# Out-projection of a macaron block in three f16 terms, with contexts split on two engines and routed stores spread over pairs

## The chip, the cores and the metric

The kernel runs on one core of one Trainium2 chip. The time is that of the device, in microseconds (us), median of several runs. The core has a TensorE (PE; its weight loads are listed as PEld), a VectorE (DVE), a ScalarE (ACT), a GpSimd (POOL) and queues for DMA (SP issues most of them). Each engine runs its own instructions in order; semaphores join them.

## The reference, cut to what matters

x has 4 x 512 tokens of 128 numbers. A switch feed-forward layer (8 experts), an attention of 16 heads and the same feed-forward layer again are added to it one after the other:

```
x = x + 0.5 * ffn(layernorm(x))
x = x + attn(layernorm(x))
x = x + 0.5 * ffn(layernorm(x))

# attn, for each of the 4 sequences of 512 tokens
q, k, v = (tanh(x @ W + b) for W, b in ((Wq, bq), (Wk, bk), (Wv, bv)))   # 16 heads of 64
alpha = softmax(where(causal, q @ k.T / 8, -inf))
ctx = alpha @ v                         # all heads side by side: 1024 numbers a token
attn = tanh(ctx @ Wo + bo)              # the out-projection, 1024 -> 128

# ffn
e = argmax(x @ gate_w.T); each expert keeps its first 320 tokens
ans = prob * (relu(x @ w1[e] + b1[e]) @ w2[e] + b2[e])
```

## The kernel before

The span has three stages: the first feed-forward layer (up to about 104 us), the attention (about 110 to 412 us) and the second feed-forward layer. The change is in the attention.

The attention goes over 4 batches b (one sequence of 512 tokens each) and in each over 8 pairs of heads r, so over 32 pairs i = 8b + r. `step(b, r)` exists on each of four engines, written out by hand; a pair is worked on in a pipeline over four steps. In step i:

- PE makes q and k of pair i (`kq`, line 695, three f16 terms: high weights times high x, low times high, high times low), then, where the step has one, the extra work `early`, then the scores of pair i-1 (`scores`, lines 719 and 726), the first half of the contexts of pair i-2 (`context`, lines 758 to 760), v of pair i (lines 705, 706), the transposes of the contexts of pair i-3 (`context_t`, line 554) into the PSUM bank `tT`, and the second half of the contexts of pair i-2.
- ACT does the tanh of q and k, the f16 high half of v (`v_high`), the three exponentials of pair i-1 (`exps`, line 501), the tanh of v, and copies `tT` as f32 into `CT` (`copy_ct`, line 505).
- DVE rounds the exponentials to f16 (`p_high`, line 1085), divides the contexts of pair i-2 by their denominators (`normalise`, lines 1095 and 1099; the denominator is a 65th column of the contexts, made by a column of ones in `Vh`) and makes the low halves of two of the three exponentials (`p_low`, line 1090).
- POOL makes the low half of v (`v_low`) and of the first exponential (`p_low`), both line 360.

There is one bank `tT`, and several things pass through it. Who wants to write into it calls `tt_free(t)`, which waits until `ct_ready` has counted the reading of the transposed contexts of all pairs before t. In step i both `context_t` and, much earlier in the step, `early` wait so, with t = i-3. The `early` work is: in batch 0, steps r = 1, 3, 5, the transposes of the next batch's normalised x (`norm_x`; at r = 1 without the wait); in batches 1 to 3, at r = 3 the out-projection of the batch before (`project_out`, line 775: eight f32 matmuls of 128x128 weights on 512 columns), at r = 4 the transposes of its tanh (`turn_out`, line 783), at r = 6 the transposes of its normalised rows (`turn_batch`, line 554). The last batch has its out-projection behind the last step, in pieces of six, one and one pair.

Beside the pairs, DVE adds the attention's output to x and measures it (r = 4), normalises it (r = 5) and chooses experts (r = 7; ranks and places in r = 0 and r = 1 of the next batch). POOL stores the routed rows of batch b-2 into the dispatch buffer in step r = 3 of batch b = 2 and 3, four indirect DMAs (`dispatch`, line 329) between its `v_low` and its `p_low`; the other two batches are stored behind the steps.

Of the kernel before, what the change touches and what calls it, by code (L numbers as in the profile page):

```python
# [68 lines left out]
B1_COL, BQ_COL, BK_COL, BO_COL, GW_COL, B2_COL, ROWS = 0, 32, 40, 48, 49, 57, 65  # L69
# [18 lines left out]
def macaron(nc, x_d, wq, bq, wk, bk, wv, bv, wo, bo, gate_w, w1, b1, w2, b2, out):  # L88
    ctx = ExitStack()
    with ctx:  # L90
        def sb(name, shape, dt):
            return ctx.enter_context(nc.sbuf_tensor(name, shape, dt))
# [4 lines left out]
        def sem(name):  # L97
# [5 lines left out]
        disp = [nc.dram_tensor(f"disp{k}", [SLOTS + NTOK, ROW], F32, kind="Internal").ap() for k in range(2)]  # L103
# [8 lines left out]
        XN = sb("XN", [P, NT, ROW], F32)  # L112
# [5 lines left out]
        Wf = sb("Wf", [P, 4096], F32)  # L118
# [5 lines left out]
        RT = sb("RT", [P, ROWS], F32)  # L124
# [40 lines left out]
        idx = sb("idx", [P, NT], U32)  # L165
# [11 lines left out]
        am = sb("am", [P, 8], F32)  # L177
        Tq = [sb(f"Tq{u}", [P, GN], F32) for u in range(2)]
        Tk = [sb(f"Tk{u}", [P, GN], F32) for u in range(2)]
        Vh = [sb(f"Vh{u}", [P, GT, 2, HD + 1], F16) for u in range(2)]  # L180
# [7 lines left out]
        bvr, bvt, bvu = Pf0[:, 0, 0:1024], Ph0[:, 0, 0:1024].bitcast(BF16), Ph0[:, 1, 0:1024].bitcast(BF16)  # L188
        rden = [sb(f"rden{h}", [P, GT], F32) for h in range(2)]
        cn = [sb(f"cn{u}", [P, GT, P], F32) for u in range(2)]  # L190
        CT = sb("CT", [P, NPAIR, GN], F32)
        yT = sb("yT", [P, GN], F32)

        SC = ctx.enter_context(nc.psum_tensor("sc", [P, 4, 512], F32))
# [1 line left out]
        pj0, pj1, cx, tT = bank("pj0"), bank("pj1"), bank("cx"), bank("tT")  # L196
# [6 lines left out]
            w1_in0 w1_in1 w2_in0 w2_in1 xe_ps xe_ready h_ps h_ready y_ps yt_ready back_ps y_ready y_sc0 y_sc1  # L203
            combined passed amax amax_all wscale bv_ready w_split w_ready
            q_ps k_ps v_ps tq tk tv v_hi v_lo
            s_ps exp_done p_hi p_lo_v p_lo_p ctx_ps rden_ready ctxn ct_ps ct_ready wo_ps yt yt_ps x_added
            x_hi x_lo""".split()
        S = {n: sem(n) for n in names}
        w1_in, w2_in = [S["w1_in0"], S["w1_in1"]], [S["w2_in0"], S["w2_in1"]]
# [80 lines left out]
        def _(pool):  # L290
# [32 lines left out]
            def dispatch(n, phase, first_tile, tiles):  # L323
                pool.wait_ge(S["idx_ready"], n + 1)
                pool.sem_inc(S["passed"], 1)
                for t in range(tiles):
                    if n == NS - 1 and first_tile + t == NT - 1:
                        pool.sem_inc(S["nearly"], 1)
                    pool.indirect_dma_start(disp[phase], bass.IndirectOffsetOnAxis(ap=idx[:, first_tile + t:first_tile + t + 1], axis=0),  # L329
                                            XN[:, first_tile + t, :], None).then_inc(S["scattered"], 16)  # L330
# [17 lines left out]
            pool.memset(bvf[:], 0.0).then_inc(S["bv_zero"], 1)  # L348
            pool.memset(bvs[:], 0.0).then_inc(S["bvs_zero"], 1)
            for u in range(2):  # L350
                pool.memset(Vh[u][:, :, :, HD:HD + 1], 1.0)
            pool.wait_ge(S["slots_empty"], 16)
            for k, (t0, tiles) in enumerate(FIRST):
                dispatch(k, 0, t0, tiles)
# [11 lines left out]
            def p_low(s, u):  # L366
                pool.wait_ge(S["p_hi"], 3 * s + 1)
                low(Pl[u][:, :, 0:GN], Pf[u][:, :, 0:GN], Ph[u][:, :, 0:GN], S["p_lo_p"])

            def step(b, r, score=True, between=None):  # L370
                i, u = NPAIR * b + r, r % 2
                if score:
                    v_low(i - 1, 1 - u)
                if between:
                    between()
                if score:
                    p_low(i - 1, 1 - u)

            def batch_inv_std(b):
                inv_std(NS + NG + b, 0, GT)  # L380

            def batch_dispatch(b):
                dispatch(NS + b, 1, GT * b, GT)

            inv_std(NS, 0, GT)
            inv_std(NS + 1, 0, GT)
# [5 lines left out]

            for b in range(2, NG):
                for r in range(NPAIR):
                    step(b, r, between={3: lambda: batch_dispatch(b - 2), 4: lambda: batch_inv_std(b - 1)}.get(r))
            step(NG, 0)
            batch_dispatch(NG - 2)
            batch_inv_std(NG - 1)
# [6 lines left out]
        def _(act):  # L405
# [96 lines left out]

            def copy_ct(t, r):
                act.wait_ge(S["ct_ps"], t + 1)
                act.activation(CT[:, r, :], tT[:], ACT.Copy).then_inc(S["ct_ready"], 1)

            def out_tanh(b, ps):
                act.wait_ge(S["wo_ps"], b + 1)
                act.activation(yT[:], ps[:], ACT.Tanh, bias=RT[:, BO_COL:BO_COL + 1]).then_inc(S["yt"], 1)

            def step(b, r, project=True, score=True, turn=True, between=None):
                i, u = NPAIR * b + r, r % 2
# [15 lines left out]
            for b in range(1, NG):  # L528
                between = {3: lambda: out_tanh(b - 1, tT), 6: lambda: copy_xt(NG - 1 + b, 0, tT),
                           7: lambda: exp_logits(NS - 1 + b, 0, GT)}  # L530
# [12 lines left out]
        def _(pe):  # L543
            mm = nc.tensor.matmul
# [136 lines left out]
            TERMS = ((0, 0), (1, 0), (0, 1))  # L681
# [89 lines left out]
            def project_out(b, ps, first=0, end=NPAIR):  # L771

                tt_free(NPAIR * b + end)
                for r in range(first, end):
                    last = mm(ps[:], Wf[:, 3072 + P * r:3072 + P * r + P], CT[:, r, :], start=r == 0, stop=r == NPAIR - 1)  # L775
                if end == NPAIR:
                    last.then_inc(S["wo_ps"], 1)

# [86 lines left out]
        def _(dve):  # L865
# [121 lines left out]
            def scale_weights(s):  # L987
                dve.wait_ge(S["amax_all"], 1)
                s.done(dve.tensor_scalar(am[:, 2:3], am[:, 1:2], 1e-30, None, ALU.max))
                s.done(dve.tensor_scalar(am[:, 3:4].bitcast(U32), am[:, 2:3].bitcast(U32), 0x7F800000, None, ALU.bitwise_and))  # L990
                s.done(dve.reciprocal(am[:, 6:7], am[:, 3:4]))
                s.done(dve.tensor_scalar(am[:, 4:5], am[:, 6:7], 2.0 ** 14, None, ALU.mult))
                s.done(dve.tensor_scalar(am[:, 5:6], am[:, 3:4], 2.0 ** -14, None, ALU.mult))
                s.end()

            dve.memset(carry[:], 0.0).then_inc(S["carry0"], 1)
# [35 lines left out]
            dve.memset(carry[:], 0.0).then_inc(S["carry0"], 1)  # L1032

            dve.wait_ge(S["w_in"], 64)
            s = Steps(dve, S["wscale"], 0, 8)
            s.done(dve.tensor_reduce(am[:, 0:1], Wf[:], X_AXIS, ALU.max))
            s.done(dve.tensor_reduce(am[:, 6:7], Wf[:], X_AXIS, ALU.min))
            s.done(dve.tensor_scalar(am[:, 7:8], am[:, 6:7], -1.0, None, ALU.mult))
# [5 lines left out]
            s = Steps(dve, S["bv_ready"], 0, 8)  # L1044
# [42 lines left out]
            def p_low(s, u, c):  # L1087
                at = scored(s, u, c)[0]
                dve.wait_ge(S["p_hi"], 3 * s + c + 1)
                dve.tensor_tensor(Pl[u][:, :, at], Pf[u][:, :, at], Ph[u][:, :, at], ALU.subtract).then_inc(S["p_lo_v"], 1)  # L1090

            def normalise(c, u, h):
                heads = cx[:, 0:GT * (HD + 1)].rearrange("p (t d) -> p t d", d=HD + 1)
                dve.wait_ge(S["ctx_ps"], 2 * c + h + 1)
                dve.reciprocal(rden[h][:], heads[:, :, HD]).then_inc(S["rden_ready"], 1)
                if h == 0 and not (isinstance(c, int) and c < 2):
                    dve.wait_ge(S["ct_ps"], c - 1)
                dve.wait_ge(S["rden_ready"], 2 * c + h + 1)
                dve.tensor_tensor(cn[u][:, :, HD * h:HD * h + HD], heads[:, :, 0:HD],  # L1099
                                  rden[h][:].unsqueeze(2).broadcast_to([P, GT, HD]), ALU.mult).then_inc(S["ctxn"], 1)  # L1100

            def step(b, r, score=True, mix=True, between=None):
                i, u = NPAIR * b + r, r % 2
                if between:
                    between()
                if score:
                    p_high(i - 1, 1 - u, 0)
                if mix:
                    normalise(i - 2, u, 0)
                if score:  # L1110
                    p_high(i - 1, 1 - u, 1)
                if mix:
                    normalise(i - 2, u, 1)
                if score:
                    p_low(i - 1, 1 - u, 1)
                    p_high(i - 1, 1 - u, 2)
                    p_low(i - 1, 1 - u, 2)

            def add_out(b):

                dve.wait_ge(S["yt_ps"], b + 1)
                xg = X[:, bass.ds(GT * b, GT), :]
                dve.tensor_tensor(xg, xg, tT[:].rearrange("p (t d) -> p t d", d=P), ALU.add).then_inc(S["x_added"], 1)
                dve.wait_ge(S["x_added"], b + 1)
# [5 lines left out]
            for r in range(NPAIR):  # L1130
                def between():
                    if r in X_STATS:
                        x_stats(X_STATS[r])
                    if r in X_TURN:
                        x_low(X_TURN[r])
                    if r in X_APPLY:
                        x_apply(X_APPLY[r])

                step(0, r, score=r > 0, mix=r > 1, between=between)
            dve.wait_ge(S["carry0"], 2)  # L1140

            def batch_stats(b):
# [18 lines left out]
            step(NG, 0, between=lambda: take_ranks(s, NS + NG - 2, GT * (NG - 2), 0, GT, cx))  # L1161
            place(s, GT * (NG - 2), 0, GT)
            normalise(NPAIR * NG - 1, 1, 0)
            normalise(NPAIR * NG - 1, 1, 1)
            add_out(NG - 1)
            batch_stats(NG - 1)
            norm_batch(NG, NG - 1)
# [26 lines left out]
```

## Time and profile before

| | us |
|---|---|
| time before, median of 3 runs | 488.85 (487.86 to 491.42) |
| the profiled execution, its time | 491.53 |
| its span | 489.8 |
| PE busy | 402.5 (82%) |
| DVE busy | 305.4 (62%) |
| ACT busy | 244.9 (50%) |
| POOL busy | 214.6 (44%) |

The span is the time from the first instruction to the last; what lies around it makes up the rest of the execution's time. Shares of busy time are averages over the three stages.

### The profile page before, as it was taken

How to read it: one execution, taken by the hardware profiler on the slowest of the kernel's cores; microseconds unless marked ns; L12 is line 12 of the kernel's file. 1: busy time of each engine (PE TensorE's matmuls, PEld its weight loads, DVE VectorE, ACT ScalarE, POOL GpSimd, SP SyncE). 2: the span in 40 equal slices, each digit the busy share in tenths (PEclk: the TensorE clock that was granted, in tenths of full speed). 3: DMA queues.
4: the chain of work that ended last, by engine and by line, in shares of the span. 5: the costliest groups of instructions: out<-in, count | busy, mean ns of one | idle time of the engine just before them, and what ended most of it. 6: DMA issues, size and time to landing. Idle time of an engine off the chain costs nothing.

```text
span 489.8 us, 11094 instructions
## 1 busy us (share of the span) xinstructions
PE 402.5 (82%) x4555; PEld 299.9 (61%) x4555; DVE 305.4 (62%) x734; ACT 244.9 (50%) x361; POOL 214.6 (44%) x173
## 2 busy tenths in 40 slices
PE   2645999428889999999999978999989988489990
PEld 1432677204667888587878666878577854237760
DVE  5883243655899877479898289798289892301210
ACT  1100454204767788387777456777467731016440
POOL 6463045620544453154434273534174524202787
PEclk9997699855999999999999999999999999779995
DMA  7913343161000000000000010000010001044643
GB/s 219 333 50 90 99 138 107 42 206 81 1 3 2 3 3 2 1 24 2 3 1 3 5 40 3 1 3 3 0 47 1 3 1 44 13 112 120 132 73 28
DMA packets 29194, 24.98 MB, mean 51 GB/s; under 512 B 3082, under 2 KB 25665, under 8 KB 28888
## 3 DMA queue, kind: packets, MB, share of 16 engines
q1 hardware_dynamic: 23008, 17.91, 12.4%
q0 software_dynamic: 4544, 4.22, 4.3%
q10 hardware_dynamic: 1592, 2.14, 1.2%
q8 instruction: 36, 0.59, 0.5%
q14 instruction: 14, 0.11, 0.1%
HBM read 15.29 MB, written 9.51 MB: 51 GB/s over the span
## 4 chain that ended last, share of the span: by engine, by line
PE 52%; DVE 26%; issue 8%; POOL 7%; DMA 4%; ACT 1%; ACTq 1%; SPq 0%; DVEq 0%; POOLq 0%
DVE Pl L1090 7%; PE sc L726 7%; DVE Ph L1085 7%; PE sc L596 7%; PE pj L695 6%; PE tT L775 4%; PE pj L605 4%; PE cx L758 4%; POOL out L342 3%; PE cx L760 3%; PE cx L759 3%; PE pj L705 3%; PE tT L554 3%; POOL disp L329 2%; PE pj L726 2%
## 5 line engine op out<-in xcount | busy, mean ns | idle before, releaser
L726 PE MATMUL sc<-Tq,Tk 64*128 64x128 f32 (+2 forms) x640 | 78.6, 345 | 0.0
L758 PE MATMUL cx<-Vh,Ph 128*128 128x65 f16 x640 | 65.1, 195 | 14.8 <-DVE Pl L1090 7.3
L758 PEld LDWEIGHTS cx<-Vh,Ph 128*128 128x128 f16 x640 | 58.2, 97 | 21.3 <-DVE cn L1099 7.5
L726 PEld LDWEIGHTS sc<-Tq,Tk 64*128 64x128 f32 x640 | 62.3, 187 | 11.6
L1085 DVE CAST Ph<-Pf 128x1024 f16<-128x1024 f32 (+1 forms) x48 | 49.7, 1036 | 31.4 <-ACT Pf L501 31.2
L759 PE MATMUL cx<-Vl,Ph 128*128 128x64 f16 x640 | 64.8, 193 | 0.0
L760 PE MATMUL cx<-Vh,Pl 128*128 128x65 f16 x640 | 64.6, 193 | 0.0
L759 PEld LDWEIGHTS cx<-Vl,Ph 128*128 128x128 f16 x640 | 58.6, 98 | 0.3
L760 PEld LDWEIGHTS cx<-Vh,Pl 128*128 128x128 f16 x640 | 58.7, 97 | 0.0
L428 ACT ACTIVATE hT<-sc,RT 128x320 f32<-128x320 f32 x64 | 33.7, 527 | 44.7 <-PE sc L596 44.0
L360 POOL TENSOR_TENSOR Vl<-Tv,Vh 128x512 f16<-128x512 f32 x16 | 19.4, 1213 | 74.0 <-ACT Vh L493 74.0
L1085 DVE CAST Ph<-Wf 128x1024 f16<-128x1024 f32 (+1 forms) x48 | 45.5, 948 | 5.8 <-ACT Wf L501 5.8
L329 POOL DMA_INDIRECT disp<-XN,idx x32 | 32.7, 1020 | 29.2 <-DVE idx L939 15.9
L596 PE MATMUL sc<-xeT,W 128*128 128x320 f32 x128 | 43.1, 486 | 2.7 <-DVE xeT L951 1.6
L360 POOL TENSOR_TENSOR Pl<-Wf,Ph 128x1024 f16<-128x1024 f32 x16 | 34.7, 2166 | 19.8 <-DVE Ph L1085 19.8
L360 POOL TENSOR_TENSOR Pl<-Pf,Ph 128x1024 f16<-128x1024 f32 x16 | 34.4, 2152 | 17.8 <-DVE Ph L1085 17.6
L479 ACT ACTIVATE Tk<-pj,RT,am 128x512 f32<-128x512 f32 x32 | 24.9, 778 | 33.2 <-PE pj L695 33.2
L501 ACT ACTIVATE Wf<-sc,pshift 128x1024 f32<-128x1024 f32 x32 | 35.6, 1114 | 10.3 <-PE sc L726 7.6
L1090 DVE TENSOR_TENSOR Pl<-Pf,Ph 128x1024 f16<-128x1024 f32 (+1 forms) x32 | 39.0, 1220 | 0.6
L549 PE MATMUL cx<-lower,onesb 128*128 128x512 bf16 x58 | 20.0, 519 | 23.4 <-DVE ve L880 14.0
L726 PE MATMUL pj<-Tq,Tk 64*128 64x128 f32 x256 | 38.8, 272 | 0.0
L963 DVE TENSOR_TENSOR Y<-cx,XE 128x256 f32<-128x256 f32 x16 | 6.8, 424 | 51.0 <-PE cx L616 40.5
(196 smaller groups left out, 1028.9 us busy)
## 6 DMA issues: line engine op xcount, KB each, us to landing
W<-in_L_ffn_w SPq DMA_DIRECT2D x32, 256.0 KB, 2.7
disp<-empty SPq DMA_DIRECT2D x2, 1300.0 KB, 7.6
XE<-disp SPq DMA_DIRECT2D x16, 130.0 KB, 2.3
ytok<-empty SPq DMA_DIRECT2D x1, 1024.0 KB
G<-ytok SPq DMA_DIRECT2D x4, 256.0 KB, 3.4
out<-X SPq DMA_DIRECT2D x4, 256.0 KB
XR<-disp SPq DMA_DIRECT2D x16, 32.5 KB, 2.0
X<-in_L_attn_states SPq DMA_DIRECT2D x2, 256.0 KB, 3.2
```

The lines of the kernel that those rows point to most:

```text
L329: pool.indirect_dma_start(disp[phase], bass.IndirectOffsetOnAxis(ap=idx[:, first_tile + t:first_tile + t + 1], axis=0), XN[:, first_tile + ...
L360: pool.tensor_tensor(dst, src, hi, ALU.subtract).then_inc(done, 1)
L428: act.activation(hT[e % 2][:, ft, :], hbank[ft][:, 0:CAP], ACT.Relu, bias=RT[:, B1_COL + k:B1_COL + k + 1]).then_inc(S["h_ready"], 1)
L501: act.activation(Pf[u][:, :, at], source, ACT.Exp, scale=0.125, bias=pshift[:]).then_inc(S["exp_done"], 1)
L596: mm(hbank[ft][:, 0:CAP], W1[e % 2][:, P * ft:P * ft + P], xeT[e % 2][:], start=True, stop=True).then_inc(S["h_ps"], 1)
L695: last = mm(ps[:], wpart(w, wl, r), (XL if xl else XH)[:, bass.ds(GN * b, GN)], start=t == 0, stop=t == 2)
L726: m = mm(score_bank(h, c)[:, o + x:o + y], Tk[u][half(h), q:q + P], Tq[u][half(h), q + x:q + y], start=False, stop=last and (c, h) != (2, 0))
L758: mm(cx[:, o:o + HD + 1], Ph[u][:, h, a:a + P], Vh[u][:, kt, h, :], start=kt == 0, stop=False)
L759: mm(cx[:, o:o + HD], Ph[u][:, h, a:a + P], Vl[u][:, kt, h, :], start=False, stop=False)
L760: last = mm(cx[:, o:o + HD + 1], Pl[u][:, h, a:a + P], Vh[u][:, kt, h, :], start=False, stop=kt == qt)
L1085: dve.tensor_copy(Ph[u][:, :, at], Pf[u][:, :, at]).then_inc(S["p_hi"], 1)
L1090: dve.tensor_tensor(Pl[u][:, :, at], Pf[u][:, :, at], Ph[u][:, :, at], ALU.subtract).then_inc(S["p_lo_v"], 1)
```

## The change

Four things are changed, all in the attention.

1. The out-projection uses the f16 halves of its weights (`WH`, `WL`, which are scaled by a power of two and are made anyway) in three terms, 24 f16 matmuls of 512 columns in place of 8 f32 ones for each batch.
2. The transposed contexts are split: ACT copies `tT` into an f16 buffer `CTH` and counts `ct_hi`; DVE then subtracts it from `tT` into an f16 buffer `CTL` (`ct_low`) and only that counts `ct_ready`. There is one `ct_low` for each of the 32 pairs, at the end of DVE's step.
3. The column of ones in `Vh` becomes 1/1024, so that contexts are 1024 times larger; the tanh of the out-projection takes a scale that undoes both factors, a column of `am` made by one more small DVE instruction.
4. The four routed stores of a batch are issued one each in steps 2, 3, 4 and 5, behind `p_low`, and no longer together in step 3 ahead of it.

```diff
-        CT = sb("CT", [P, NPAIR, GN], F32)
+        CTH = sb("CTH", [P, NPAIR, GN], F16)
+        CTL = sb("CTL", [P, NPAIR, GN], F16)
...
-                pool.memset(Vh[u][:, :, :, HD:HD + 1], 1.0)
+                pool.memset(Vh[u][:, :, :, HD:HD + 1], 1.0 / CTX_SCALE)
...
                 if score:
                     p_low(i - 1, 1 - u)
+                if behind:
+                    behind()
...
+            def dispatch_tile(b, t):
+                if t == 0:
+                    pool.wait_ge(S["idx_ready"], NS + b + 1)
+                at = GT * b + t
+                pool.indirect_dma_start(disp[1], bass.IndirectOffsetOnAxis(ap=idx[:, at:at + 1], axis=0),
+                                        XN[:, at, :], None).then_inc(S["scattered"], 16)
...
-                    step(b, r, between={3: lambda: batch_dispatch(b - 2), 4: lambda: batch_inv_std(b - 1)}.get(r))
+                    step(b, r, between=(lambda: batch_inv_std(b - 1)) if r == 4 else None,
+                         behind=(lambda: dispatch_tile(b - 2, r - 2)) if 2 <= r < 2 + GT else None)
...
-                act.activation(CT[:, r, :], tT[:], ACT.Copy).then_inc(S["ct_ready"], 1)
+                act.activation(CTH[:, r, :], tT[:], ACT.Copy).then_inc(S["ct_hi"], 1)
...
-                act.activation(yT[:], ps[:], ACT.Tanh, bias=RT[:, BO_COL:BO_COL + 1]).then_inc(S["yt"], 1)
+                act.activation(yT[:], ps[:], ACT.Tanh, bias=RT[:, BO_COL:BO_COL + 1], scale=am[:, 7:8]).then_inc(S["yt"], 1)
...
-                    last = mm(ps[:], Wf[:, 3072 + P * r:3072 + P * r + P], CT[:, r, :], start=r == 0, stop=r == NPAIR - 1)
+                    for k, (wl, cl) in enumerate(TERMS):
+                        last = mm(ps[:], wpart(3, wl, r), (CTL if cl else CTH)[:, r, :],
+                                  start=(r, k) == (0, 0), stop=(r, k) == (NPAIR - 1, 2))
...
+            def ct_low(t):
+                dve.wait_ge(S["ct_hi"], t + 1)
+                dve.tensor_tensor(CTL[:, t % NPAIR, :], tT[:], CTH[:, t % NPAIR, :], ALU.subtract).then_inc(S["ct_ready"], 1)
+
...
                     p_low(i - 1, 1 - u, 2)
+                if turn:
+                    ct_low(i - 3)
...
             normalise(NPAIR * NG - 1, 1, 0)
+            ct_low(NPAIR * NG - 2)
             normalise(NPAIR * NG - 1, 1, 1)
+            ct_low(NPAIR * NG - 1)
             add_out(NG - 1)
```

How the instructions of DVE stand in steps r = 3 and r = 4 of batch 1, from the second `p_high` of step 3 to the addition of the attention's output, before:

```order
L1085 CAST Ph<-Pf 128x2x512 [waits ctx_ps,exp_done]
L1095 RECIPROCAL rden<-cx 128x4 [waits ctx_ps]
L1099 TENSOR_TENSOR cn<-cx,rden 128x4x64 [waits rden_ready]
L1090 TENSOR_TENSOR Pl<-Pf,Ph 128x2x512 [waits p_hi]
L1085 CAST Ph<-Pf 128x2x256 [waits ctx_ps,exp_done]
L1090 TENSOR_TENSOR Pl<-Pf,Ph 128x2x256 [waits p_hi]
L1123 TENSOR_TENSOR X<-X,tT 128x512 [waits yt_ps]
L871 MEMSET spare 128x1 [waits x_added]
```

and with the change:

```order
L1100 CAST Ph<-Pf 128x2x512 [waits ctx_ps,exp_done]
L1110 RECIPROCAL rden<-cx 128x4 [waits ctx_ps]
L1114 TENSOR_TENSOR cn<-cx,rden 128x4x64 [waits rden_ready]
L1105 TENSOR_TENSOR Pl<-Pf,Ph 128x2x512 [waits p_hi]
L1100 CAST Ph<-Pf 128x2x256 [waits ctx_ps,exp_done]
L1105 TENSOR_TENSOR Pl<-Pf,Ph 128x2x256 [waits p_hi]
L1119 TENSOR_TENSOR CTL<-tT,CTH 128x512 [waits ct_hi]
L1144 TENSOR_TENSOR X<-X,tT 128x512 [waits yt_ps]
L885 MEMSET spare 128x1 [waits x_added]
```

The subtraction into `CTL` is the last instruction of the step, behind both low halves. PE waits for `ct_ready` at the out-projection (r = 3 of batch 1), here before:

```order
L695 MATMUL pj<-XH,WL 128x512
L695 MATMUL pj<-XL,WH 128x512
L775 MATMUL tT<-CT,Wf 128x512 [waits ct_ready]
L775 MATMUL tT<-CT,Wf 128x512 x7
L719 MATMUL sc<-maskn,identb 128x128 [waits exp_done]
```

and with the change:

```order
L707 MATMUL pj<-XH,WL 128x512
L707 MATMUL pj<-XL,WH 128x512
L788 MATMUL tT<-CTH,WH 128x512 [waits ct_ready]
L788 MATMUL tT<-CTH,WL 128x512
L788 MATMUL tT<-CTL,WH 128x512
L788 MATMUL tT<-CTH,WH 128x512
```

The wait stands at the same place, behind `kq` and ahead of the scores; what signals it is now the last instruction of DVE's step. POOL in steps r = 2 to 5 of batch 2, before:

```order
L360 TENSOR_TENSOR Pl<-Wf,Ph 128x2x512 [waits p_hi]
L360 TENSOR_TENSOR Vl<-Tv,Vh 128x512 [waits v_hi]
L329 DMA disp<-XN,idx 4608x130 [waits idx_ready]
L329 DMA disp<-XN,idx 4608x130 x3
L360 TENSOR_TENSOR Pl<-Pf,Ph 128x2x512 [waits p_hi]
L360 TENSOR_TENSOR Vl<-Wf,Vh 128x512 [waits v_hi]
L321 TENSOR_TENSOR r<-ve,mhalf 128x4 [waits var_ready]
L360 TENSOR_TENSOR Pl<-Wf,Ph 128x2x512 [waits p_hi]
```

and with the change:

```order
L362 TENSOR_TENSOR Pl<-Wf,Ph 128x2x512 [waits p_hi]
L393 DMA disp<-XN,idx 4608x130 [waits idx_ready]
L362 TENSOR_TENSOR Vl<-Tv,Vh 128x512 [waits v_hi]
L362 TENSOR_TENSOR Pl<-Pf,Ph 128x2x512 [waits p_hi]
L393 DMA disp<-XN,idx 4608x130
L362 TENSOR_TENSOR Vl<-Wf,Vh 128x512 [waits v_hi]
L323 TENSOR_TENSOR r<-ve,mhalf 128x4 [waits var_ready]
L362 TENSOR_TENSOR Pl<-Wf,Ph 128x2x512 [waits p_hi]
L393 DMA disp<-XN,idx 4608x130
```

Nothing stands between `v_low` and `p_low` of step 3 any more.

## Rows read from the trace of the kernel before

**Rows 1.** Busy time by stretch: from:to, length, each engine's busy us, granted clock, DMA.

```profile
153.10:236.30 83.20, 82.68 (x1252) 66.32 (x1249) 62.01 (x111) 61.11 (x83) 36.07 (x22) 1.00 0.02 5
236.30:310.80 74.50, 68.69 (x1019) 54.56 (x1016) 58.87 (x112) 48.75 (x67) 33.52 (x21) 1.00 0.03 9
```

**Rows 2.** Chain of waits: start, us, work; out-projections and the kq three steps later.

```profile
199.57 6.87 PE tT L775 x16
...
228.52 1.29 PE pj L695 x6
...
269.65 6.87 PE tT L775 x16
...
303.01 1.30 PE pj L695 x6
...
344.14 6.87 PE tT L775 x16
...
375.60 1.29 PE pj L695 x6
```

**Rows 3.** Instruction groups by shape: count, busy us, mean ns, idle before.

```profile
L775 PE MATMUL tT<-CT,Wf 128*128 128x512 f32 x48 | 21.1, 592 | 0.0
L695 PE MATMUL pj<-XL,WH 128*128 128x512 f16 x64 | 25.3, 395 | 0.0
L1073 DVE TENSOR_TENSOR XL<-tT,XH 128x512 f16<-128x512 f32 x4 | 2.7, 687 | 4.4 <-ACT XH L456 4.4
L456 ACT ACTIVATE XH<-tT 128x512 f16<-128x512 f32 x4 | 2.4, 595 | 20.0 <-PE tT L554 19.9
```

**Rows 4.** Timeline (start, duration) at the out-projection of batch 1: ACT, PE, DVE.

```profile
197.54 0.59 ACT L505 ACTIVATE CT<-tT 128x512 f32<-128x512 f32 x1
199.41 0.59 PE L775 MATMUL tT<-CT,Wf 128*128 128x512 f32 x1
200.46 0.69 DVE L1090 TENSOR_TENSOR Pl<-Wf,Ph 128x512 f16<-128x512 f32 x1
```

**Rows 5.** Timeline at step r = 6 of batch 1, and its step 5 ahead.

```profile
223.10 1.49 POOL L360 TENSOR_TENSOR Vl<-Tv,Vh 128x512 f16<-128x512 f32 x1 [1.64 <-ACT Vh L493]
223.53 1.08 DVE L888 TENSOR_TENSOR ra<-r 128x4 f32<-128x4 f32 x1
231.57 0.69 DVE L1090 TENSOR_TENSOR Pl<-Pf,Ph 128x512 f16<-128x512 f32 x1
229.65 0.60 PE L554 MATMUL tT<-identf,XN 128*128 128x128 f32 x4
```

**Rows 6.** Timeline at the routed stores of batch 2, r = 3: POOL, DVE, PE.

```profile
279.14 1.20 POOL L329 DMA_INDIRECT disp<-XN,idx  x1 [0.19 <-issue]
...
283.40 1.86 POOL L329 DMA_INDIRECT disp<-XN,idx  x1 [0.30 <-issue]
284.80 4.26 DVE L1090 TENSOR_TENSOR Pl<-Pf,Ph 128x512 f16<-128x512 f32 x1
285.29 2.14 POOL L360 TENSOR_TENSOR Pl<-Pf,Ph 128x1024 f16<-128x1024 f32 x1
289.32 0.19 PE L758 MATMUL cx<-Vh,Ph 128*128 128x65 f16 x1 [2.13 <-DVE Pl L1090]
```

**Rows 7.** Timeline at step r = 5 of batch 0: PE, then DVE.

```profile
154.30 0.38 PE L554 MATMUL tT<-identf,xa 128*128 128x128 f32 x2
...
156.22 0.69 DVE L1090 TENSOR_TENSOR Pl<-Wf,Ph 128x512 f16<-128x512 f32 x1
156.83 0.68 DVE L1073 TENSOR_TENSOR XL<-tT,XH 128x512 f16<-128x512 f32 x1
```

**Rows 8.** The tail: chain piece of the last out-projection, then timeline of DVE and PE.

```profile
399.63 5.23 PE pj L775 x12
...
402.03 0.69 DVE L1090 TENSOR_TENSOR Pl<-Wf,Ph 128x512 f16<-128x512 f32 x1
...
410.18 0.70 PE L775 MATMUL pj<-CT,Wf 128*128 128x512 f32 x1 [0.69 <-ACT CT L505]
```

**Rows 9.** Busy time by stretch, columns as in the first group.

```profile
116.00:122.00 6.00, 5.64 (x35) 3.85 (x35) 3.49 (x19) 2.89 (x5) 0.00 (x0) 0.55 0.00 0
416.00:422.00 6.00, 2.96 (x25) 1.90 (x23) 2.98 (x15) 0.83 (x2) 0.12 (x1) 0.99 0.01 3
422.00:428.00 6.00, 1.79 (x11) 0.66 (x8) 1.75 (x13) 0.00 (x0) 2.56 (x3) 0.50 0.08 24
```

More of the change, by code:

```diff
@@ L59 @@
 ROUTE_STEPS = 12
+CTX_SCALE = 2.0 ** 10
 KOFF = [0, 512, 1024, 896]
@@ L205, in macaron @@
             q_ps k_ps v_ps tq tk tv v_hi v_lo
-            s_ps exp_done p_hi p_lo_v p_lo_p ctx_ps rden_ready ctxn ct_ps ct_ready wo_ps yt yt_ps x_added
+            s_ps exp_done p_hi p_lo_v p_lo_p ctx_ps rden_ready ctxn ct_ps ct_hi ct_ready wo_ps yt yt_ps x_added
             x_hi x_lo""".split()
@@ L368, in p_low, with step @@
                 low(Pl[u][:, :, 0:GN], Pf[u][:, :, 0:GN], Ph[u][:, :, 0:GN], S["p_lo_p"])
-            def step(b, r, score=True, between=None):
+            def step(b, r, score=True, between=None, behind=None):
                 i, u = NPAIR * b + r, r % 2
@@ L993, in scale_weights @@
                 s.done(dve.tensor_scalar(am[:, 5:6], am[:, 3:4], 2.0 ** -14, None, ALU.mult))
+                s.done(dve.tensor_scalar(am[:, 7:8], am[:, 5:6], 1.0 / CTX_SCALE, None, ALU.mult))
                 s.end()
@@ L1034, in _ @@
             dve.wait_ge(S["w_in"], 64)
-            s = Steps(dve, S["wscale"], 0, 8)
+            s = Steps(dve, S["wscale"], 0, 9)
             s.done(dve.tensor_reduce(am[:, 0:1], Wf[:], X_AXIS, ALU.max))
@@ L1100, in normalise, with step @@
                                   rden[h][:].unsqueeze(2).broadcast_to([P, GT, HD]), ALU.mult).then_inc(S["ctxn"], 1)
-            def step(b, r, score=True, mix=True, between=None):
+            def ct_low(t):
+                dve.wait_ge(S["ct_hi"], t + 1)
+                dve.tensor_tensor(CTL[:, t % NPAIR, :], tT[:], CTH[:, t % NPAIR, :], ALU.subtract).then_inc(S["ct_ready"], 1)
+            def step(b, r, score=True, mix=True, turn=True, between=None):
                 i, u = NPAIR * b + r, r % 2
@@ L1137, in between @@
                         x_apply(X_APPLY[r])
-                step(0, r, score=r > 0, mix=r > 1, between=between)
+                step(0, r, score=r > 0, mix=r > 1, turn=r > 2, between=between)
             dve.wait_ge(S["carry0"], 2)
```

## The prediction

> **What bounds the kernel now.** I read the busy time by stretch first. In the stretch that holds most of batches 0 and 1, PE is busy 82.7 of 83.2 us at a granted clock of 1.00, in the next 68.7 of 74.5 [rows 1]. So in batches 0 and 1 every wait that PE gets in the attention is paid in full, and in batches 2 and 3 nearly so. The chain of waits says where the rest went: from the start of the out-projection to `kq` of step 6 it takes 28.95 us in batch 1 (199.57 to 228.52), 33.36 in batch 2 and 31.46 in batch 3 [rows 2]. The work is the same but for the routed stores, so these cost 4.4 and 2.5 us. How they do it stands in the timeline: POOL's `p_low` comes late, behind the four stores, and then runs from 285.29 to 287.43; DVE's last low half, which takes 0.69 us elsewhere, takes 4.26 and ends at 289.06; PE waits 2.13 us for it [rows 6].
>
> Last I looked at who frees `tT`. At the out-projection of batch 1 PE starts at 199.41 straight behind `kq`; ACT's copy of the bank had ended at 198.13, but DVE's step ends only at 201.15 [rows 4]. That is the place the change touches.
>
> **The change, part by part.**
>
> *The matmuls.* Eight f32 matmuls take 6.87 us [rows 2], 0.86 each. An f16 one of the same shape: six of `kq` take 1.29 us [rows 2], 0.215 each, so 24 take 5.2. Gain 1.7 for each of batches 0 to 2, 5.1 in all. In the tail the first six f32 ones take 5.23 [rows 8] and 18 f16 ones 3.9, gain 1.3; the last pair gains 0.2 to 0.3.
>
> *ACT.* The copy into f16 takes 595 ns [rows 3], into f32 0.59 us [rows 4]: nothing. The tanh keeps its form but for a column as scale, the small DVE instruction for that column comes in the first expert stage, once: 0 to 0.2 us, I take nothing. The constant in `Vh` costs nothing.
>
> *`ct_low` as work on DVE.* Its form (one operand in PSUM, one f16 in SBUF, 512 columns, f16 out) is in the trace: 687 ns [rows 3], and the next instruction follows 0.61 us after the start of one that takes 0.69 [rows 7]. 30 of the 32 go on the end of DVE's steps. DVE is busy 62.0 of 83.2 us [rows 1], so most of them lie in idle time. Where DVE is itself late, at r = 7, 0 and 1 (expert choice, ranks, places), I count 0.5 us at each of the two batch boundaries and 0.6 at the tail: the small two-operand instructions there are held by POOL as `ra` is at r = 5, 1.08 us until POOL's subtraction has ended [rows 5], and what is issued 0.6 later is held 0.6 less.
> What would change this is `ct_low` being held by POOL too; the 687 ns are a mean over only four. The Trainium skill (GPSIMD Engine Reference, Specifications) says that the interface to SBUF is shared with VectorE for instructions in a two-port mode or with two SBUF inputs; by that `ct_low`, with one input in PSUM, is free of it, and the trace agrees with 687 ns.
>
> *`ct_low` as what frees `tT`.* PE's early work now waits for the end of DVE's previous step plus one subtraction. Each place, from the end of DVE's last low half (next start 0.08 before that end), plus 0.69, plus 0.04 for the signal:
> - r = 3, batch 1: last low half starts at 200.46, `ct_low` at 201.07, ends 201.76, PE at 201.80 instead of 199.41 [rows 4]: 2.4 us. In batches 2 and 3 DVE comes out of its late stretch, 2.7 each. Sum 7.8.
> - r = 4, three times. After the wait at r = 3 the scores are as late as PE is, so DVE's step starts as late, and nothing of the wait has been used up: again 2.4 each, 7.2.
> - r = 6, three times. DVE's step 5 is longer by the normalising: last low half at 231.57, `ct_low` from 232.18 to 232.87, PE at 232.91 instead of 229.65 [rows 5]: 3.3 each, 9.8.
> - r = 5 of batch 0: DVE runs without a gap there, so the `ct_low` of step 3 comes on top: 156.22 + 0.61, then `ct_low` from 157.44 to 158.13; PE at 158.17 instead of 154.30 [rows 7]: 3.9. At r = 3 of batch 0 nothing has to be freed yet.
> - tail: the first six terms wait for the `ct_low` of the last full step: 402.03 + 0.6 + 0.61, to 403.93; PE at 403.97 instead of 399.47 [rows 8]: 4.5, of which 0.6 is the boundary above.
> - last pair: PE already waits 0.69 for ACT's copy [rows 8]; a `ct_low` of 0.69 and its signal come behind the copy, less 0.3 for the faster matmuls: +0.4.
>
> In each case the queue behind the wait is PE's whole step, scores first; ACT, DVE and POOL live on those scores, so the wait shifts all four engines and nobody catches it up.
>
> *The routed stores.* Moved behind `p_low`, they give back the 4.4 and 2.5 us. POOL is idle 1.64 us ahead of its `v_low` even at r = 5 [rows 5], and a store takes 1.2 to 1.9 us of it [rows 6]; as a store may push `v_low` onto DVE's normalising at r = 5, I take 0.4 off for each batch: gain 4.0 and 2.1. Bounds: nothing, and 6.9.
>
> *Sum.* Waits 7.8 + 7.2 + 9.8 + 3.9 + 4.5 + 0.4 = 33.6; batch boundaries 2 x 0.5 = 1.0; matmuls -5.1 - 1.3 = -6.4; stores -6.1. Total +22. On the profiled execution 491.53 + 22.1 = 513.6; that execution lies 2.7 above the median of its kernel, so the median should come to 488.85 + 22.1 = 511.0.
>
> **The rivals.**
>
> *A. The waits are there, and the clock falls too.* PE gets gaps of 2.4 to 4.5 us, where batch 2's largest so far was 2.13 [rows 6]. The clock is granted at 0.99 from 416 to 422 us, where PE is busy 2.96 of 6 us, and at 0.50 behind [rows 9]; so a few thin microseconds are enough somewhere. Against it: the stretch 236 to 311 holds gaps too and stays at 1.00 [rows 1]. The price: with PE busy 5.64 of 6 us, the clock is still 0.55 from 116 to 122 [rows 9], after a start at 112.8, so that stretch alone loses 0.45 x 6 = 2.7 us, and one fall costs 3 us or more. Three falls give about 520. The Trainium skill (TensorE: Matmul & The Clock Gate, Part 1) has the same rule, that an idle engine goes back to 1.2 GHz and has to be busy for a while to get 2.4 again; by it the longest gaps, at r = 6, at r = 5 of batch 0 and in the tail, are those at risk. Chance 0.18.
>
> *B. The waits are half as long.* If DVE's step were to get shorter once PE is late (its `p_high` is held by POOL's `p_low`, which could drift apart), each wait would shrink, by up to 1 us of ten: about 501. Against it: the collision follows from the first `p_high`, which starts both. Chance 0.1.
>
> *C. The other sign: the bank is not missed.* If DVE's step ended ahead of PE's early work, only the gains would stand: 488.85 - 6.4 - 6.1 + about 1.6 at the boundaries = 478. It turns on one comparison, DVE's step end plus 0.7 against PE's `kq` end; it would need DVE to be 2.4 us earlier at r = 3 and 3.3 at r = 6. The trace has it at 201.15 against 199.41, in PE-bound steps that repeat. Chance 0.04.
>
> **How the numbers follow.** Forecast 0.68, A 0.18, B 0.1, C 0.04. The forecast's own range is 506 to 518: stores between nothing and 6.9 us of gain move it by +6 to -1, the boundaries by 1, and each of the eleven waits may be off by 0.3. The range given goes from 501 (B in) to 521 (three falls of the clock). One per cent of the time is about what a measurement of this kernel tells from no change: slower by over 1% holds the forecast, A and B, 0.95; same 0.02 and faster 0.03 share C.
>
> **What would show it.** In the changed profile: PE's first `project_out` and `turn_out` matmuls and the `turn_batch` transposes idle 2.4, 2.4 and 3.3 us with DVE's `CTL` subtraction as releaser, once per batch; about 4 us ahead of the last out-projection; eleven such gaps and about 33 us in all. Out-projection of a batch 5.2 us. `ct_low` 0.69 us each whatever POOL does. The long 4.26 us low half gone. From `project_out` to `kq` of step 6 batches 2 and 3 as long as batch 1. I am wrong if PE's idle ahead of the early work names something else or is under 1 us; if the clock row has a 0.5 inside the attention, it is A.

## The result, and the profile after

| | before | changed |
|---|---|---|
| time, median of 4 runs | 488.36 (487.31 to 491.42) | 525.12 (522.87 to 529.37) |
| span of the profiled execution | 489.8 | 523.2 |
| attention: first `kq` to the transposes of the last out-projection | 299.8 | 336.4 |
| the same without its start (see below) | 270.2 | 309.0 |

The ratio is 1.075 (95% interval 1.067 to 1.084). By the medians the change makes the kernel 36.8 us slower. The two profiled executions are 33.4 us apart; their attentions differ by 36.6, and the rest of the span is 3.2 shorter in the changed one. The direction was forecast, the size was not: 511 was forecast, with a range that ended at 521.

The attention begins at half clock, and the moment at which the clock rises differs between executions. So its start, from the first `kq` to the first transposes of contexts (`cn`), takes different times with the same 294 matmuls, here in before, in the changed kernel and in the run fill below (length, busy us of PE, PEld, DVE, ACT, POOL, then clock, DMA share, GB/s):

```profile
112.70:142.30 29.60, 25.70 (x294) 18.57 (x294) 23.19 (x67) 19.70 (x26) 10.82 (x8) 0.85 0.01 3
111.00:138.40 27.40, 23.42 (x294) 17.01 (x294) 23.15 (x67) 19.55 (x26) 10.69 (x8) 0.95 0.01 2
110.70:140.70 30.00, 26.07 (x294) 18.93 (x294) 23.24 (x67) 19.70 (x26) 11.21 (x8) 0.84 0.01 2
```

Nothing that any of the kernels changes on this path has begun there, but for POOL's order in three of them. What a kernel costs is therefore read behind the start: 309.0 against 270.2, 38.8 us.

Who waited for whom, PE's waits for DVE's subtraction in the changed kernel (total us, times, longest):

```profile
PE tT L566 <- DVE CTL L1119: 12.4, 4, 3.1
...
PE tT L788 <- DVE CTL L1119: 7.5, 3, 2.6
...
PE tT L797 <- DVE CTL L1119: 6.7, 3, 2.2
PE pj L788 <- DVE CTL L1119: 5.2, 2, 3.8
```

None of these lines exists before. Twelve waits, 31.8 us, at the forecast places. The chain of waits goes through them; here the three steps of batch 1 that have one, r = 3, 4 and 6 (start, us, work):

```profile
202.71 0.69 DVE CTL L1119
203.54 5.34 PE tT L788 x24
...
217.86 0.61 DVE CTL L1119
218.51 0.66 PE tT L797 x4
...
238.34 0.69 DVE CTL L1119
239.07 0.66 PE tT L566 x4
```

The out-projection takes 5.34 us for 24 matmuls, where [rows 2] had 6.87 for the 8 f32 ones (each stands as two records in that row). The subtraction itself is as cheap as [rows 3] said. Its line, over all 32 (min/median/max ns):

```profile
L1119 DVE TENSOR_TENSOR CTL<-tT,CTH x32: 676/683/690, 145.2 to 444.6; 128x512 f16<-128x512 f32 x32
```

What the sum did not have is in the granted clock, the third column from the end:

```profile
158.00:218.40 60.40, 55.95 (x862) 44.25 (x860) 43.41 (x70) 42.39 (x57) 22.42 (x14) 1.00 0.01 2
218.40:224.00 5.60, 5.49 (x55) 4.60 (x56) 2.85 (x14) 1.47 (x2) 1.77 (x3) 0.70 0.16 47
239.00:244.30 5.30, 5.22 (x46) 4.30 (x47) 0.71 (x2) 2.32 (x4) 1.12 (x1) 0.68 0.00 0
284.30:291.40 7.10, 7.06 (x29) 3.01 (x30) 0.00 (x0) 0.04 (x1) 0.00 (x0) 0.76 0.00 0
432.60:439.30 6.70, 6.63 (x20) 2.68 (x21) 1.02 (x8) 0.00 (x0) 3.79 (x4) 0.61 0.09 30
111.00:447.40 336.40, 289.55 (x4088) 223.80 (x4089) 241.93 (x497) 196.99 (x269) 125.46 (x82) 0.94 0.02 7
```

```profile
219.60:223.62 4.02, 4.02 (x31) 3.30 (x31) 2.40 (x13) 1.11 (x1) 1.01 (x1) 0.60 0.22 65
209.26:211.72 2.46, 2.46 (x32) 2.08 (x31) 0.10 (x1) 2.07 (x3) 1.12 (x1) 1.00 0.00 0
```

Ten of the eleven waits over 2 us have such a stretch behind them; only the one at 203.5 has none. Before, the attention had no fall of the clock once the first pairs were under way, not behind its 2.13 us of [rows 6] either; this is all of it behind the start:

```profile
142.30:412.50 270.20, 254.08 (x3762) 200.97 (x3763) 207.56 (x399) 177.06 (x243) 118.38 (x75) 1.00 0.03 8
```

### The profile page after: what moved, and what is told of

Read it like the earlier page. It is cut to its first block, busy times and chain, and to the rows that moved or that the text cites. A ratio compares the mean times of both kernels' runs of the same rounds, so it can differ in the third digit from the quotient of the medians.

```text
span 523.2 us, 11189 instructions
## 1 busy us (share of the span) xinstructions
PE 407.5 (78%) x4587; PEld 302.1 (58%) x4587; DVE 316.8 (61%) x767; ACT 245.1 (47%) x361; POOL 210.8 (40%) x173
## 3 DMA queue, kind: packets, MB, share of 16 engines
q1 hardware_dynamic: 23008, 17.91, 11.8%
## 4 chain that ended last, share of the span: by engine, by line
PE 42%; DVE 34%; issue 10%; POOL 6%; DMA 4%; ACT 2%; ACTq 1%; SPq 0%; DVEq 0%; POOLq 0%
DVE Ph L1100 11%; DVE Pl L1105 10%; PE sc L738 8%; PE sc L608 6%; PE pj L617 4%; PE tT L788 4%; POOL out L344 3%; DVE CTL L1119 3%; PE cx L770 3%; PE tT L566 2%; PE pj L707 2%; PE cx L772 2%; PE cx L771 2%; POOL disp L331 2%; PE pj L738 2%
## 5 line engine op out<-in xcount | busy, mean ns | idle before, releaser
L738 PE MATMUL sc<-Tq,Tk 64*128 64x128 f32 (+2 forms) x640 | 86.3, 372 | 0.0
L738 PEld LDWEIGHTS sc<-Tq,Tk 64*128 64x128 f32 x640 | 67.7, 204 | 14.6 <-issue 5.5
L608 PE MATMUL sc<-xeT,W 128*128 128x320 f32 x128 | 39.6, 454 | 2.7 <-DVE xeT L965 1.6
L738 PE MATMUL pj<-Tq,Tk 64*128 64x128 f32 x256 | 40.2, 278 | 0.0
L513 ACT ACTIVATE Pf<-sc,pshift 128x1024 f32<-128x1024 f32 x32 | 35.2, 1111 | 7.2 <-PE sc L738 5.0
L362 POOL TENSOR_TENSOR Vl<-Wf,Vh 128x512 f16<-128x512 f32 x16 | 18.4, 1150 | 45.9 <-ACT Vh L505 45.9
L617 PE MATMUL pj<-hT,W 128*128 128x320 f32 x128 | 36.8, 433 | 0.0
```

The source lines that it names most:

```text
L362: pool.tensor_tensor(dst, src, hi, ALU.subtract).then_inc(done, 1)
L513: act.activation(Pf[u][:, :, at], source, ACT.Exp, scale=0.125, bias=pshift[:]).then_inc(S["exp_done"], 1)
L608: mm(hbank[ft][:, 0:CAP], W1[e % 2][:, P * ft:P * ft + P], xeT[e % 2][:], start=True, stop=True).then_inc(S["h_ps"], 1)
L617: last = mm((pj0, pj1)[e % 2][:, 0:CAP], W2[e % 2][:, ft, :], hT[e % 2][:, ft, :], start=ft == 0, stop=ft == FT - 1)
L738: m = mm(score_bank(h, c)[:, o + x:o + y], Tk[u][half(h), q:q + P], Tq[u][half(h), q + x:q + y], start=False, stop=last and (c, h) != (2, 0))
```

## The experiments

Fourteen kernels beside the two were tried in five groups; three that bear on one point each are told in a sentence, and the others are in the table. Each group ran on one chip with the kernel before, whose median was between 486.6 and 493.2 there; so times are compared by their ratio, and the attention of the one profiled execution by its length. The table gives both, and in the last column the attention behind its start.

| kernel | median, before beside it | ratio (95%) | attention | behind the start |
|---|---|---|---|---|
| before | 488.4 | 1 | 299.8 | 270.2 |
| changed | 525.1, 488.4 | 1.075 (1.067 to 1.084) | 336.4 | 309.0 |
| fill | 513.3, 487.1 | 1.052 (1.044 to 1.059) | 322.0 | 292.0 |
| low_mid | 497.3, 487.1 | 1.024 (1.016 to 1.031) | 306.8 | 278.1 |
| no_low | 475.7, 487.1 | 0.977 (0.971 to 0.983) | 286.5 | 256.7 |
| stores_only | 480.5, 487.1 | 0.986 (0.980 to 0.992) | 291.6 | 264.1 |
| stores_back | 532.0, 493.2 | 1.077 (1.070 to 1.085) | 343.0 | 313.1 |
| early_late | 502.2, 493.2 | 1.017 (1.009 to 1.024) | 314.2 | 284.5 |
| work_only | 479.6, 486.6 | 0.988 (0.981 to 0.994) | 291.7 | 264.2 |
| wait_only | 510.0, 486.6 | 1.048 (1.041 to 1.056) | 324.5 | 295.8 |
| wait_fill | 505.2, 486.6 | 1.039 (1.034 to 1.045) | 317.4 | 287.5 |
| mid_swap | 481.8, 488.3 | 0.988 (0.981 to 0.996) | 292.4 | 265.5 |
| stores_swap | 481.5, 493.0 | 0.982 (0.973 to 0.991) | 292.2 | 265.3 |

**Theory clock:** the forecast's sum holds, and the time above it is matmuls at half clock behind the waits. **Theory work:** the sum is wrong elsewhere; DVE's 30 more subtractions cost more than the batch boundaries.

### Filler in the waits

```diff
+            def fill(i, count):
+                pe.wait_ge(S["exp_done"], 3 * (i - 1))
+                for k in range(count):
+                    mm(sc[k % 4], onesb[:], lower[:].unsqueeze(1).broadcast_to([P, GT, P]), start=True, stop=True)
...
+                    if turn and i > 3:
+                        fill(i, {3: 10, 4: 9, 5: 13, 6: 13}[r])
                     if turn:
                         tt_free(i - 3)
```

> The changed kernel, with filler: ahead of each wait for the freed bank (r = 3, 4, 6 of batches 1 to 3, r = 5 of batch 0, tail) PE runs 9 to 14 bf16 matmuls of 512 columns into score banks that are free then; they are overwritten. The waits stay, only PE is busy in them. Theory clock: of the time lost, some 17 us are matmuls run at half clock just behind each wait (in the trace of the changed kernel the scores behind a wait take 3.2 to 4.0 us against 2.46 elsewhere, the out-projection 6.7 to 7.0 against 5.3, the tail's 6.6 against 3.9); with filler the granted clock stays 1.00 in the attention and the time falls from 525 to about 508. Theory work: the loss beyond the waits is DVE's added work and collisions; then the time stays at 525 (up to 2 more for the filler).

The attention takes 322.0 us, 14.4 less, and the whole 11.8 less. But here the start took 30.0 us and in the changed kernel 27.4; behind it 292.0 are left of 309.0, 17.0 less. The changed kernel with the waits filled:

```profile
110.70:432.70 322.00, 301.83 (x4211) 228.19 (x4212) 243.16 (x497) 197.18 (x269) 126.25 (x82) 0.99 0.02 7
203.00:224.00 21.00, 20.54 (x240) 13.98 (x239) 10.24 (x27) 9.70 (x13) 6.22 (x5) 1.00 0.05 14
```

The clock stays up (the 0.99 is the start of the attention, before the clock has risen), and nothing else became faster: DVE still frees the bank last, PE only works meanwhile. Theory clock holds for 17.0 us, 1.7 for each of ten falls. What is left is 292.0 - 270.2 = 21.8 us above the kernel before.

### The wait without the work

```diff
                     if turn:
                         tt_free(i - 3)
+                    if turn and i > 3:
+                        pe.wait_ge(S["p_lo_v"], 2 * (i - 2) + 2)
                     early()
```

This is the kernel before with spread stores, f32 out-projection and no subtraction; only the early work (and the last out-projection) waits for DVE's last low half.

> The wait without the work and without any f16 term: the kernel before with spread stores (attention 291.6 us, 480.5 in all), whose early work at r = 3, 4, 6, at r = 5 of batch 0 and in the tail waits in addition for DVE's last low half of the step before. The waits come out of the trace of before: 1.8 us at r = 3 and r = 4 (six), 2.65 at r = 6 and at r = 5 of batch 0 (four), 3.3 in the tail, 24.7 in all. Theory clock: some falls of the clock come on top, 1.5 us each; attention 316 plus up to 12. Without falls, 316.

> As wait_only, with 7 to 13 filler matmuls ahead of each wait, so that PE is not idle in it. Theory clock: granted clock 1.00 throughout the attention, which takes 291.6 + 24.7 = 316, whatever wait_only took beyond that goes away. Were the rest of wait_only's loss something else, both take the same.

wait_only takes 324.5 us in the attention, wait_fill 317.4, against 316 from the rows of the kernel before. Behind the start it is 295.8 and 287.5, against 264.1 in stores_only, the same kernel without the waits. So the waits are 23.4 us, forecast 24.7 (PE's idle times at the eleven places add up to 23.5), and the clock costs another 8.3, again 1.7 for each fall. Here it fell five times, behind the waits of 2.5 us at r = 6 and at r = 5 of batch 0 and of 3.2 in the tail, and never behind the six of 1.7 at r = 3 and 4. The mean clock of the whole attention, and of a stretch in it:

```profile
110.30:434.80 324.50, 288.71 (x4055) 223.88 (x4056) 223.60 (x465) 197.29 (x269) 126.96 (x82) 0.96 0.02 8
158.00:236.00 78.00, 72.87 (x1094) 57.17 (x1090) 53.82 (x99) 52.55 (x71) 29.33 (x18) 1.00 0.02 5
```

The second stretch holds the first waits of 1.7 us, at 202.4 and 218.6, and its clock is 1.00.

### The work without the wait, and the gain alone

no_low leaves the subtraction out, and with it the low halves of the contexts, and lets ACT's copy free the bank:

```diff
-                act.activation(CTH[:, r, :], tT[:], ACT.Copy).then_inc(S["ct_hi"], 1)
+                act.activation(CTH[:, r, :], tT[:], ACT.Copy).then_inc(S["ct_ready"], 1)
...
-                        last = mm(ps[:], wpart(3, wl, r), (CTL if cl else CTH)[:, r, :],
+                        last = mm(ps[:], wpart(3, wl, r), CTH[:, r, :],
```

> The changed kernel without the subtraction into CTL; the high halves stand in for the low ones in the third term, and ACT's copy frees the bank as before. It leaves out the low halves of the contexts. All else (24 f16 matmuls, spread stores, scale) is as changed. Both theories: this is the gain alone, 6.4 us of matmuls and up to 6.9 of stores, time 488.4 - 6.4 - 6.1 = about 476; were it at 485 or more, the gains that the prediction counted would be smaller than said.

Measured 475.7 and an attention of 286.5: behind the start, the gain of the change without its subtraction is 13.5 us (forecast 12.5). work_only adds to no_low, at the place of each subtraction in a step, an instruction that frees nothing:

```diff
+                dve.tensor_reduce(busy[:, t:t + 1], G[:, 0:GT, :].rearrange("p t d -> p (t d)"), X_AXIS, ALU.max)
```

> Takes the two jobs of the subtraction apart: the work without the wait. The changed kernel, but ACT's copy frees the bank as before, and at the place of each subtraction DVE runs a maximum over 512 f32 numbers of SBUF, with one input, about as long. It leaves out the low halves of the contexts, as no_low does (attention there 286.5 us, start of the first kq to the transposes of the last out-projection). Theory wait: the work is hidden but for the batch boundaries, attention 287 to 289. Theory work: 30 x 0.6 = 18 us more, attention above 295.

It takes 677 ns each and 291.7 us in the attention, 5.2 more than no_low; behind the start it is 264.2, 7.5 more. Neither theory had that number: more than half of the work is hidden (7.5 of 30 x 0.61 = 18 us shows), but it costs over four times the 1.6 us counted for the boundaries. The changed kernel has about the same work on DVE and takes 309.0. So about 45 us of its loss come from who frees the bank and not from the work: the waits, and the clock behind them.

### The stores

stores_only is the kernel before with the fourth part of the change alone; stores_back is the changed kernel without it:

```diff
-                    step(b, r, between=(lambda: batch_inv_std(b - 1)) if r == 4 else None,
-                         behind=(lambda: dispatch_tile(b - 2, r - 2)) if 2 <= r < 2 + GT else None)
+                    step(b, r, between={3: lambda: batch_dispatch(b - 2), 4: lambda: batch_inv_std(b - 1)}.get(r))
```

> The kernel before with the routed stores of batches 0 and 1 spread over r = 2 to 5 behind p_low, nothing else. As the prediction counts them: 4.0 + 2.1, time 482.3. Rival: the stores collide with other work and the gain is under 2 us.

> The changed kernel with its routed stores together again in r = 3 of batches 2 and 3, ahead of p_low. By the prediction's terms they cost 6.1 us, 525.1 + 6.1 = 531; alone on the kernel before they cost 6.6. Rival: here PE waits at r = 4 in any case, so the stores hide behind that wait, and the time stays at 525 to 527.

Alone, the spread stores take 8.2 us off the attention, of which 2.1 are the earlier rise of the clock in its start and 6.1 the stores, and 1.4% (0.8 to 2.0) off the whole. Undone in the changed kernel they put 6.6 back in the attention, 336.4 to 343.0, but only 4.1 behind the start, 309.0 to 313.1, and by their ratios, 1.075 and 1.077, the two kernels can't be told apart. The clock fell eight times in stores_back and ten times in the changed kernel, which at 1.7 us each hides some 3 us; what the stores cost in the changed kernel is open between 4 and 8. The rival, that PE's wait at r = 4 hides them, is at least not the whole: the late low half of [rows 6] makes the subtraction late too, and PE waits up to 3.8 us for it there:

```profile
PE tT L796 <- DVE CTL L1118: 8.4, 3, 3.8
```

This line is of stores_back; with spread stores the same three waits are 6.7 us, the longest 2.2.

### Moving the subtraction

low_mid puts it ahead of the two low halves of DVE's step:

```diff
                 if mix:
                     normalise(i - 2, u, 1)
+                if turn:
+                    ct_low(i - 3)
                 if score:
                     p_low(i - 1, 1 - u, 1)
...
                     p_low(i - 1, 1 - u, 2)
-                if turn:
-                    ct_low(i - 3)
```

> The changed kernel, with the subtraction into CTL ahead of the two low halves of DVE's step (behind both normalisings) and no longer at its end. Same work on every engine. Theory order (the loss is that the bank is freed at the end of DVE's step): the waits shrink from 2.3 to about 0.2 us at r = 3 and 4, from 3.1 to about 1 at r = 6, 3.1 to 1.6 at r = 5 of batch 0, tail 3.8 to about 2.3; the clock falls less often; time about 486 to 490. Theory work (30 more subtractions are what DVE can't carry): the low halves come 0.6 later in each step and PE waits for them instead; time still above 510.

306.8 us in the attention (278.1 behind the start, 31 less) and 497.3 in all, 7 to 11 more than expected. PE now waits for something else, in low_mid:

```profile
PE cx L770 <- DVE Pl L1105: 10.6, 13, 1.5
```

Thirteen waits, also in ordinary steps. One of them, DVE then POOL then PE:

```profile
186.19 1.49 DVE L1105 TENSOR_TENSOR Pl<-Wf,Ph 128x512 f16<-128x512 f32 x1
...
185.95 1.18 POOL L362 TENSOR_TENSOR Vl<-Tv,Vh 128x512 f16<-128x512 f32 x1 [2.97 <-ACT Vh L505]
...
187.94 0.19 PE L770 MATMUL cx<-Vh,Ph 128*128 128x65 f16 x1 [0.52 <-DVE Pl L1105]
```

DVE's last low half, 0.6 us later than before, now starts inside POOL's `v_low` and takes 1.49 us in place of the 0.69 of [rows 4]; it ends 0.55 after POOL. The subtraction into `CTL`, with one operand in PSUM, keeps its 676 to 690 ns whatever POOL does, here beside a `v_low` in the changed kernel:

```profile
172.82 1.13 POOL L362 TENSOR_TENSOR Vl<-Tv,Vh 128x512 f16<-128x512 f32 x1 [3.18 <-ACT Vh L505]
172.88 0.68 DVE L1119 TENSOR_TENSOR CTL<-tT,CTH 128x512 f16<-128x512 f32 x1
```

So the place at the end of the step was free of this and late for the bank, the place ahead of the low halves the reverse. Putting it ahead only in the steps whose end PE's early work waits for (low_some, expected 494 to 495) took 498.1. Whether it helped stays open: by its ratio, 1.009 against 1.024, it did; by the one attention behind the start, 277.6 against 278.1, it did not. The waits in ordinary steps went, as expected (5.0 us in 7 are left of 10.6 in 13), but waits for the normalising grew from 4.8 to 8.9 us.

early_late leaves DVE alone and moves PE's early work of batches 1 to 3 behind the scores, and ACT's part of it behind the exponentials; here PE's:

```diff
                 if score:
                     scores(i - 1, 1 - u, project)
+                if early and b:
+                    tt_free(i - 3)
+                    early()
```

> The changed kernel with DVE's order untouched (subtraction at the end), but in batches 1 to 3 PE's early work (out-projection, its transposes, transposes of the rows) stands behind the scores, and ACT's part of it (tanh, copy) behind the exponentials. The scores take 3.1 us from the end of kq, so the bank is free by then. Theory order: 9 of the 11 waits (23 us) and the falls of the clock behind them (some 12 us) go; left are 3.1 at r = 5 of batch 0 and 3.8 + 1.4 in the tail; time about 488 to 492. Theory work: above 505.

Six waits for the bank went and the three at r = 6 shrank from 3.1 to 1.0 us; left are these, with what took part of their place:

```profile
PE cx L773 <- DVE cn L1120: 10.2, 11, 1.6
PE tT L569 <- DVE CTL L1125: 6.1, 4, 3.1
PE pj L791 <- DVE CTL L1125: 5.2, 2, 3.8
PE cx L773 <- DVE Pl L1111: 5.1, 7, 1.2
```

314.2 us and a ratio of 1.017, which is 496.5 on a kernel before of 488.4, against 488 to 492 expected. DVE now waits for the later transposes at r = 4 before it can go on with its step, and PE waits for the normalising (10.2 us). With the subtraction moved as well in two steps (late_mid, expected 483 to 487) the median was 498.5, the ratio 1.009, the attention 306.5.

### The collision taken away

mid_swap is low_mid with POOL's `v_low` behind its `p_low`, so that it runs while DVE works on operands in PSUM (the normalising and the subtraction into `CTL`):

```diff
-                if score:
-                    v_low(i - 1, 1 - u)
                 if between:
                     between()
                 if score:
                     p_low(i - 1, 1 - u)
+                    v_low(i - 1, 1 - u)
                 if behind:
```

> The run with the subtraction ahead of the low halves (low_mid, attention 306.8 us, of which PE waits 10.6 for DVE's last low half), and in addition POOL's v_low stands behind its p_low. Theory collision (those waits come from v_low starting with DVE's last low half and holding it): v_low now runs just behind p_low, from about 168.0 to 169.1 in the clock of an ordinary step where that half starts at 171.2, so the waits in ordinary steps go and the attention falls to about 296 to 299, the whole to about 487. Theory work (DVE's step is simply too long): attention still 305 or more.

> The kernel before with spread stores (attention 291.6 us) and POOL's v_low behind its p_low, no f16 terms, no subtraction. Theory collision with the subtraction: v_low held nobody here in ordinary steps, so the gain is small, 0 to 3 us, attention 289 to 292. Rival, POOL's order pays by itself: attention falls by 8 or more, as it did from low_mid to mid_swap (14.4).

stores_swap is stores_only with POOL's order alone. In mid_swap 306.8 falls to 292.4, behind the start 278.1 to 265.5, and the waits for the last low half from 10.6 us to these, in mid_swap:

```profile
PE cx L769 <- DVE Pl L1104: 2.4, 5, 0.6
```

POOL's order by itself gives nothing: stores_swap takes 292.2 where stores_only takes 291.6, 265.3 against 264.1 behind the start. So the 12.6 us between low_mid and mid_swap come from taking the collision away (8 to 11 were expected): PE's waits for the last low half are 8.2 us shorter, those for the normalising 1.7 and those for the experts' `carry` 1.9. mid_swap is faster than the changed kernel and a little faster than before, 0.988 of it (0.981 to 0.996); stores_only, at 0.986, and stores_swap, at 0.982, can't be told from it. With the subtraction one place further ahead (first_swap, expected an attention of 288 to 290) it was 292.8: PE's waits for the bank fell from 6.6 to 4.0 us, and those for the normalising grew from 3.1 to 6.5.

## Why the prediction was wrong, point by point

- **What bounds the kernel, and who frees `tT`:** right. Every wait stands where it was put. At the out-projection of batch 1, 2.33 us (forecast 2.4), of batches 2 and 3, 2.59 each (2.7); at the turn of its tanh 2.24, 2.23, 2.24 (2.4); at r = 6 three times 3.10 (3.3); at r = 5 of batch 0, 3.10 (3.9); tail 3.83 (4.5 with the boundary), last pair 1.41 in place of 0.69 before, 0.7 more (0.4).
- **The step that failed** is the one ahead of the rivals: the sum took every matmul behind a wait at full clock, and the fall of the clock was set aside as rival A with a chance of 0.18. The row that weighed against it, a mean of 1.00 from 236 to 311 us with gaps up to 2.13 [rows 1], [rows 6], says nothing of gaps of 2.3 to 3.8; the row beside it, 0.50 behind sparse microseconds [rows 9], spoke for A and was given less weight. The clock fell ten times, for 17.0 us. A's price for one fall, 3 us or more, was nearly twice the 1.7 measured; it was taken from a start in which the clock had not yet risen. Its count, three, was less than a third of the ten.
- **The sum without the clock:** 22.1 forecast, 21.8 measured with the waits filled. Part of that agreement is luck, since the errors of the terms cancel. The waits were 31.1 us (31.8 less the 0.7 of before) against 33.0 without the boundary counted in the tail; the gain was 13.5 against 12.5; that leaves 4.2 for the subtraction as work against 1.6 counted at the boundaries and the tail. Measured alone, without the waits for the bank, the work is 7.5.
- **The matmuls:** 5.34 us for 24 in the out-projection of batch 1, forecast 5.2; in batches 2 and 3, behind falls of the clock, 6.98 and 6.74. In the tail the gain did not come: the 18 take 6.6 us at 0.61 of the clock, forecast 3.9.
- **The stores:** 6.1 us by themselves, 6.1 forecast; in the changed kernel between 4 and 8. The long low half is gone. A store of batch 2 in its new place takes 1.25 to 1.43 us on POOL.
- **Rival B** (waits half as long) and **C** (the bank is not missed): not seen. The remark that `ct_low` is held by nobody: right, 676 to 690 ns.

With A's mechanism, the ten falls and the measured 1.7 us for each, the sum would have been 22.1 + 17.0 = 39.1, against 38.8 between the two profiled executions and 36.8 between the medians.

## What to carry to other kernels

When a change adds an instruction, ask first what its end signals, and only then what it costs: here 0.69 us for each pair came to 7.5 us as work and to some 45 more as the last reader of a shared bank, because the signal moved from an engine that was early to the end of one that was late. Where a change makes TensorE idle for more than about 2 us at a time in a stretch at full clock, add the matmuls behind each wait at half clock to the sum, unless something keeps the engine busy; a few matmuls into a free bank gave back 17 of 39 us here, though the order of the instructions gave back more. And before two single executions are compared by a stage, see whether the clock rose at the same point of it: here that alone was worth up to 2.6 us. And when an instruction is put ahead of others, look at what those others will then run beside.

## What the runs showed of the hardware

The clock fell more often behind longer waits. In wait_only it fell behind none of six of 1.7 us and four of four of 2.5. Behind waits of 2.2 to 2.6 us it fell five times of six in the changed kernel, but two times of five in stores_back; in the kernel before it stayed up behind the wait of 2.13. Behind all of those of 3.1 us and more at these places it fell. The length of one wait does not decide it alone: in early_late a fall came at 424 us, behind waits of 1.55 and 1.42 us that followed each other within 4 us. A fall cost 1.7 us. The Trainium skill (TensorE: Matmul & The Clock Gate, Part 1) says that the engine goes back to 1.2 GHz when idle and regains 2.4 under steady work; by that the longest waits were those at risk, and the runs show that those of 2.2 to 2.6 us are at risk too.

A VectorE subtraction of two SBUF operands that starts inside a GpSimd subtraction ends 0.55 us after it (1.49 us in place of 0.69), one with an operand in PSUM or a reduction of one SBUF operand does not notice it (690 and 680 ns at most). The Trainium skill (GPSIMD Engine Reference, Specifications) says that its SBUF interfaces are shared with VectorE, with contention for VectorE instructions in a two-port mode or with two SBUF inputs; by it the place of the low half mattered, the place of the subtraction into `CTL` did not, and the runs agree.
